# Two phases of four samples with both layers each, in a two-layer kernel on one core

## The reference

```
# layer 0 ("layer A")
h = einsum('bij,bkj->bik', x, weight0[adapter0])     # one 1024x1024 matrix per sample
h = layernorm(h) * gamma + beta
h = fake_quant(h) @ fake_quant(w1).T + b1            # int8 grid, scale per row
h = gelu(h)
x = x + fake_quant(h) @ fake_quant(w3).T + b3
# layer 1 ("layer B")
y = x @ base_w.T + bias + scale[a] * (x @ A[a].T) @ B[a].T      # rank 16
n = y * rsqrt(mean(y*y) + eps)
res, pre, post = heads(n)                            # 16 + 4 + 4 logits per token
H = (1 - g) * I + g * sinkhorn(res, 50 iterations, tau 0.1)     # 4x4 per token
branch = sum_s softmax(pre)[s] * y[s] @ W_branch     # y as 4 streams of 256
x = x + H mixed over the 4 streams of y + branch * softmax(post)
```

## Time and profile before

| | |
|---|---|
| median of three runs | 876.65 us (874.74 to 877.16) |
| the profiled execution's own time | 874.75 us |
| its span in the trace | 872.8 us |
| mean granted TensorE clock, share of full speed | 0.954 |
| TensorE busy | 761.2 us (87%) |
| VectorE busy | 578.2 us (66%) |
| ScalarE busy | 335.4 us (38%) |
| GpSimd busy | 64.7 us (7%) |

### The profile page before, as it was taken

One profiled execution on the slowest core, in us unless ns is written; L12 is line 12 of the kernel. 1 busy time (PEld: TensorE's weight loads), 2 busy tenths in 40 slices (PEclk: granted clock), 3 DMA queues, 4 the chain that ended last, 5 costly groups with the idle time before them and its releaser, 6 DMA issues.

```text
span 872.8 us, 11055 instructions
## 1 busy us (share of the span) xinstructions
PE 761.2 (87%) x3172; PEld 488.5 (56%) x3172; DVE 578.2 (66%) x2036; ACT 335.4 (38%) x577; POOL 64.7 (7%) x34
## 2 busy tenths in 40 slices
PE   4989899989899999998968899999898892699656
PEld 2544444344444444444645788887687771587445
DVE  6555282434675656483746524438999998899998
ACT  0333733304534252434324633444333421757152
POOL 0002000202621011022020000000000000000000
PEclk9999999989999999999999899999999996899969
DMA  8994654133448353512031345334333249653103
GB/s 340 374 334 163 240 179 171 60 111 140 159 149 355 108 189 139 193 56 89 24 121 50 129 161 182 115 114 159 122 128 108 102 155 411 272 193 121 48 35 158
DMA packets 40297, 140.94 MB, mean 161 GB/s; under 512 B 8511, under 2 KB 9663, under 8 KB 34626
## 3 DMA queue, kind: packets, MB, share of 16 engines
q1 hardware_dynamic: 38962, 137.72, 43.8%
q10 hardware_dynamic: 1296, 2.74, 0.8%
HBM read 106.86 MB, written 33.58 MB: 161 GB/s over the span
## 4 chain that ended last, share of the span: by engine, by line
PE 49%; DVE 34%; ACT 8%; issue 5%; DMA 2%; POOL 1%; DVEq 0%; SPq 0%; ACTq 0%
PE PS L779 21%; PE PS L837 12%; PE PS L947 8%; DVE ksum L1361 6%; DVE kprod L1356 6%; DVE ka L1365 4%; DVE nr L1438 4%; DVE kb L1365 3%; PE PS L826 2%; ACT qT L542 2%; DVE xr L1283 2%; PE PS L868 2%; DMA x_raw<-x_tr_dram 2%; PE PS L794 1%; DVE xp L1268 1%
## 5 line engine op out<-in xcount | busy, mean ns | idle before, releaser
L779 PE MATMUL PS<-w_raw,x_raw 128*128 128x512 f32 x512 | 230.4, 604 | 13.7 <-DMA x_raw<-x_tr_dram 11.0
L779 PEld LDWEIGHTS PS<-w_raw,x_raw 128*128 128x128 f32 x512 | 96.7, 194 | 124.9 <-issue 124.1
L947 PE MATMUL PS<-w_hi,xT_hi 128*128 128x512 f32 x256 | 105.0, 410 | 0.0
L947 PE MATMUL PS<-w_lo,xT_hi 128*128 128x512 f32 x256 | 102.0, 399 | 0.0
L947 PE MATMUL PS<-w_hi,xT_lo 128*128 128x512 f32 x256 | 101.7, 397 | 0.0
L1361 DVE TENSOR_REDUCE ksum<-kprod 128x16 f32<-128x64 f32 x392 | 75.2, 233 | 0.2 <-issue 0.2
L837 PE MATMUL PS<-w3q,qT 128*128 128x512 bf16 x256 | 61.3, 395 | 14.4 <-ACT qT L542 14.4
L1131 DVE SCALAR_TENSOR_TENSOR gbuf<-PS,lnst,vecs 128x512 f32<-128x512 f32 x32 | 23.7, 749 | 75.0 <-PE PS L837 75.0
L542 ACT ACTIVATE qT<-PS,round_c 128x512 bf16<-128x512 f32 x64 | 40.3, 679 | 84.4 <-PE PS L826 84.3
L837 PE MATMUL PS<-w1q,qT 128*128 128x512 bf16 x256 | 60.4, 391 | 8.4 <-DVE x1buf L1149 5.7
L470 POOL TENSOR_TENSOR xres<-xres,vecs 128x1024 f32<-128x1024 f32 x16 | 42.2, 2659 | 329.8 <-DMA xres<-x_tok_dram 329.8
(11 more groups left out here) (165 smaller groups left out, 1128.2 us busy)
## 6 DMA issues: line engine op xcount, KB each, us to landing
w_raw<-cond_w_dram SPq DMA_DIRECT2D x32, 1024.0 KB, 5.6
stage<-w_dram SPq DMA_DIRECT2D x16, 512.0 KB, 12.1
x_raw<-x_tr_dram SPq DMA_DIRECT2D x32, 256.0 KB, 6.4
xres<-x_tok_dram SPq DMA_DIRECT2D x8, 1024.0 KB, 9.3
x_scratch<-x1buf SPq DMA_DIRECT2D x16, 512.0 KB, 6.4
x1n<-x_scratch SPq DMA_DIRECT2D x16, 512.0 KB, 5.7
xr<-x_scratch SPq DMA_DIRECT2D x16, 512.0 KB, 3.6
y_scratch<-y SPq DMA_DIRECT2D x16, 512.0 KB, 3.6
```

What stands on the lines that cost most here:

```text
L779: mm = pe.matmul(PS[:, 2 * t + h, :], x_raw[pr][:, c, t * P:(t + 1) * P], w_raw[pr][:, c, h * H2:(h + 1) * H2], start=(pr == 0 and c == 0) ...
L947: pe.matmul(PS[:, 2 * t + h, :], xx[:, c, t * P:(t + 1) * P], ws[c // 2][:, c % 2, h * H2:(h + 1) * H2], start=(c == 0 and xx is xT_hi and ...
```

## The change

The eight samples are processed as two phases of four, each with layer A, an entry and layer B (`PHASES`). What follows from that:

- **Turn.** After layer B step 3 the kernel goes back to layer A with sample 4. Before the first entry the quantised matrices `w1q` and `w3q` are stored to DRAM (`store_quantised`), and loaded again at the turn. Blocks of samples 4 and 5 are loaded as buffers of layer B come free, in the order of pairs 2, 0, 1, 3 (`ORDER`).
- **Second entry.** Samples 6 and 7 drain as before; the first entry is a copy of it with samples 2 and 3.
- **Sinkhorn of group 0** starts at the turn: 11 iterations ahead of the first layer norm, three shares of four in layer A step 5, three of three in each of steps 6 and 7, two at a time in layer B step 4. Layer B steps 5 to 7 have none. The tiles that Sinkhorn uses move to memory that layer A doesn't use.
- **Two orientations.** `kmat_t` holds the transposed matrices, and the column half of an iteration reads them, so that it multiplies and reduces with the same access pattern as the row half.
- `base_w` is loaded and split one step earlier (`GUEST`), the products of the head weights with `base_w` and the LoRA matrices (`composites_1`, `composites_2`) come one step earlier, `av_hi` and `av_lo` have 56 columns and not 128, and all loops are written out straight.

```diff
+    PHASES = ((0, HALF), (HALF, NB))
+    GUEST = 3
...
+    ORDER = (2, 0, 1, 3)
...
+        kmat_t = [sb(f"kmat_t{i}", [P, HG, NS, NS], F32) for i in range(2)]
...
+            def store_quantised():
+                sp.wait_ge(st_ev, 2 * NW)
+                for i, wq in ((0, w1q), (1, w3q)):
+                    sp.dma_start(wq_dram[i], wq[:, :, :].rearrange("p c n -> p (c n)")).then_inc(wq_st, 16)
...
+            def enter_b(ph):
+                first, end = PHASES[ph]
+                sp.wait_ge(l0_pair, PAIRS * end - 1)
...
+                    load_x1n(first, t)
+                store_x1(end - 2, 0)
+                store_x1(end - 2, 1)
+                load_xres(end - 1)
...
+                    load_x1n(first + 1, t)
+                sp.wait_ge(b_set, ph + 1)
...
+            sp.wait_ge(xt_done, 4 * HALF)
+            load_blocks(HALF, 2)
+            step_b(HALF - 1, last=True)
+            sp.wait_ge(l1_done, 4 * HALF)
+            sp.wait_ge(lg_done, HALF)
+            load_x(HALF, 2)
+            load_blocks(HALF, 0)
+            load_x(HALF, 0)
+            load_blocks(HALF, 1)
+            load_x(HALF, 1)
+            load_x(HALF, 3)
+            store_y(HALF - 1)
+            for t in range(NTOK):
+                sp.wait_ge(y_st[t], 16 * HALF)
+            sp.wait_ge(ss_done, NTOK * HALF)
+            load_blocks(HALF, 3)
+            load_w(HALF + 1, 2)
+            sp.wait_ge(wq_st, 32)
+            sp.wait_ge(br_done, HALF)
+            sp.dma_start(w1q[:, :, :].rearrange("p c n -> p (c n)"), wq_dram[0]).then_inc(w1_back, 16)
+            load_w(HALF + 1, 0)
+            store_r(HALF - 1)
+            for t in range(NTOK):
+                sp.wait_ge(r_st[t], 16 * HALF)
+            sp.dma_start(w3q[:, :, :].rearrange("p c n -> p (c n)"), wq_dram[1]).then_inc(w3_back, 16)
+            load_w(HALF + 1, 1)
+            load_w(HALF + 1, 3)
...
-                if pr == 0:
+                order = ORDER if s == HALF else range(PAIRS)
+                pe.wait_ge(wld[pr], 32 * s + 32 + (16 if s >= GUEST else 0))
+                if s == HALF and pr == order[0]:
+                    pe.wait_ge(y_ev, 4 * HALF)
+                elif pr == order[0]:
                     wait(pe, l0_evac, NTOK * s)
...
+            l0(HALF, ORDER[0])
+            branch_transposes(HALF - 1)
+            l0(HALF, ORDER[1])
+            branch(HALF - 1)
+            l0(HALF, ORDER[2])
+            l0(HALF, ORDER[3])
+            step_a(HALF + 1, w3_=False)
+            for s in range(HALF + 2, NB):
+                step_a(s)
+            enter_b(1)
+            for b in range(HALF + 1, NB):
...
+                for i in range(2):
+                    nc.vector.tensor_tensor(kmat_t[i][:, :, :, :].rearrange("p t j i -> p t i j"), hr[:, chain[i], :, :],
+                                            cols(ska[:, 1, chain[i], :], HG), ALU.mult).then_inc(k_step[i], 1)
...
+            def half(k, row):
+                vec, new = (kb, ka) if row else (ka, kb)
+                for i in range(2):
+                    v = vec[i][:, :, :]
+                    dve.wait_ge(k_step[i], k)
+                    nc.vector.tensor_tensor(kprod[i][:, :, :, :], (kmat if row else kmat_t)[i][:, :, :, :], cols(v, HG),
+                                            ALU.mult).then_inc(k_step[i], 1)
+                for i in range(2):
+                    dve.wait_ge(k_step[i], k + 1)
+                    nc.vector.tensor_reduce(ksum[i][:, :, :], kprod[i][:, :, :, :], AX.X, ALU.add).then_inc(k_step[i], 1)
+                for i in range(2):
+                    dve.wait_ge(k_step[i], k + 2)
+                    nc.vector.reciprocal(new[i][:, :, :], ksum[i][:, :, :]).then_inc(k_step[i], 1)
...
-            def half(k, row):
...
-                    nc.vector.tensor_tensor(kprod[i][:, :, :, :], kmat[i][:, :, :, :], cols(v, HG) if row else rows(v, HG),
-                                            ALU.mult).then_inc(k_step[i], 1)
...
-                    pr = kprod[i][:, :, :, :]
...
-                    nc.vector.tensor_reduce(ksum[i][:, :, :], pr if row else pr.rearrange("p t i j -> p t j i"),
-                                            AX.X, ALU.add).then_inc(k_step[i], 1)
...
+            done = [0]
+            def share(n):
+                n = min(n, SINKHORN - 1 - done[0])
+                iterations(0, done[0], n)
+                done[0] += n
+            def step_a(s, w1_=True, w3_=True, n=0):
+                if w1_:
+                    layer_norm(s - 1, 0)
...
-            def step_b(b, first=False, last=False, sink=False):
-                def share(i):
-                    if sink:
-                        n = B_ITERS // 4
-                        iterations(0, (b - NB // 2) * B_ITERS + i * n, n)
...
+                share(n)
+                if w3_:
+                    finish_w3(s - 2, 0)
+                if w1_:
+                    layer_norm(s - 1, 1)
+                if w3_:
+                    finish_w3(s - 2, 1)
+                share(n)
+                if w1_:
+                    finish_w1(s - 1, 0)
+                for first, end in PHASES:
+                    if s == end - 1:
+                        lo_xT(first, 0)
+                        lo_xT(first, 1)
+                share(n)
+                if w1_:
+                    finish_w1(s - 1, 1)
...
+            for s in range(2, HALF):
+                step_a(s)
+            enter_b(0)
+            layer_b(0)
             sinkhorn_start(0)
-            with dve.Fori(NB // 2, NB - 1) as b:
-                step_b(b, sink=True)
-            step_b(NB - 1, last=True, sink=True)
-            iterations(0, NB // 2 * B_ITERS, SINKHORN - 1 - NB // 2 * B_ITERS)
+            share(11)
+            step_a(HALF + 1, w3_=False, n=4)
+            for s in range(HALF + 2, NB):
+                step_a(s, n=3)
+            enter_b(1)
+            step_b(HALF, first=True, n=2)
+            share(SINKHORN)
             sinkhorn_finish(0)
+            for b in range(HALF + 1, NB):
+                step_b(b, last=b == NB - 1)
             lo_xp(NB - 1)
             distribute(NB - 1)
             sinkhorn_start(1)
-            with dve.Fori(0, (SINKHORN - 1) // 7) as it:
-                iterations(1, it * 7, 7)
+            iterations(1, 0, SINKHORN - 1)
```

More of the change, by code:

```diff
@@ new lines, in _ @@
+            load_stage(KC + 5)
+            load_w(1, 2)
+            load_scales(0, V_SW1)
+            load_stage(KC + 6)
+            load_stage(KC + 7)
+            load_w(1, 3)
+            load_xres(0)
+            for c in range(4):
+                load_nat(c)
+            load_w(2, 0)
+            for c in range(4, KC):
+                load_nat(c)
+            load_w(2, 1)
+            store_scales(1)
+            load_w(2, 2)
+            load_scales(1, V_SW3)
+            load_w(2, 3)
@@ new lines, in drain_a @@
+            def drain_a(end):
+                evac_T(end - 2, 0, 3)
+                ln_root(end - 1, 0)
+                quant1(end - 1, 0)
+                evac_T(end - 2, 1, 3)
+                evac_T(end - 1, 0, 1)
+                ln_root(end - 1, 1)
+                quant1(end - 1, 1)
+                evac_T(end - 1, 1, 1)
+                for t in range(NTOK):
+                    gelu(end - 1, t)
+                    quant2(end - 1, t)
+                for t in range(NTOK):
+                    evac_T(end - 1, t, 3)
@@ L1059, in mix @@
                 mm.then_inc(pm_done, 1)
+            for pr in range(PAIRS):
+                l0(0, pr)
+                stage_T(2 * pr)
+                stage_T(2 * pr + 1)
+            l0(1, 0)
+            stage_T(KC)
+            stage_T(KC + 1)
+            l0(1, 1)
+            stage_T(KC + 2)
+            stage_T(KC + 3)
+            transposes(0, 0, 1)
+            product(0, 0, 1)
+            l0(1, 2)
+            stage_T(KC + 4)
+            stage_T(KC + 5)
+            transposes(0, 1, 1)
@@ new lines, in enter_b @@
+            def enter_b(ph):
+                first, end = PHASES[ph]
+                pe.wait_ge(wlo_done, PAIRS)
+                base(first, 0, 0)
+                transposes(end - 2, 0, 3)
+                product(end - 2, 0, 3)
+                base(first, 0, 1)
+                transposes(end - 2, 1, 3)
+                product(end - 2, 1, 3)
+                transposes(end - 1, 0, 1)
+                product(end - 1, 0, 1)
+                base(first, 1, 0)
+                transposes(end - 1, 1, 1)
+                product(end - 1, 1, 1)
+                base(first, 1, 1)
+                for t in range(NTOK):
+                    transposes(end - 1, t, 3)
+                    product(end - 1, t, 3)
+                low_and_heads(first)
+                for t in range(NTOK):
+                    for h in range(2):
+                        low_rank(first, t, h)
+                heads(first)
+                x_transposes(first + 1, 0)
+                x_transposes(first + 1, 1)
@@ L1397, in step_b @@
```

(1 more changed line is left out.)

742 lines of the change are left out of this document (347 added, 395 removed).

## The result

The changed kernel takes 912.77 us (median of four runs, 911.1 to 913.54) against 875.69 us for the kernel before in the same comparison (872.34 to 877.16). The ratio is 1.0426, 95% interval 1.0391 to 1.0462: slower, as forecast. The profiled execution has a span of 909.3 us, 36.5 more than before; the sum had 26.4.

What follows compares the result with a forecast made beforehand. TensorE bounds layer A, VectorE's chain the tail; gains must come from layer B's second half, tail or an entry. Terms summed to +26.4 on span 872.8, 899.2; with 1.95 outside and 1.9 to the median, 903 us, range 889 to 914.

Steps and rivals of the forecast that it cites:

- The entry and its last step: Added entry into layer B plus phase 0's own last A step, copies of those measured: 73.4 + 6.2 = 79.6 us.
- the likeliest case: Whole kernel: the forecast itself, 903 us, with range 895 to 908 and chance 0.63.
- the heavier case: Rival, 908 to 920, chance 0.16: GpSimd lock (908), or column half gains nothing and gaps remain 1.3 (910).
- VectorE's free 18 us are in the right gaps: Layer A steps 6 and 7: nine iterations fit, only the share after lo_xT in step 7 costs, 0.9 (0 to 4).
- The turn: Layer B step 3's end back to layer A: a chain of 87.0 us, replacing two A steps of 92.0.
- slow restarts of the forecast: Turn: matmuls run slower after TensorE idles, 8.8 instead of 7.0 for l0(4, 2) and 1.8 more for a product.
- Loads due later than they land: nothing: Turn: loads of w1q, w3q and sample 5 cost nothing, unless the queue is a few us slower than 406.
- Had the iterations been free, as in that rival: Rival: group 0's 49 iterations cost no time anywhere, turn 18.1 less, 879.0 us; chance 0.07 (872 to 885).
- The transfer ahead of x1: Layer A step 3: x1n queues behind stores including wq_scratch, so transposes wait 6.0 us (0 to 7.5).
- The shares in the second entry: Second entry with layer B step 4: Sinkhorn shares delay lo_xT, gather and lo_stacks, 5.0 us (3 to 8).
- The tail: After layer B: 7.9 ahead of the iterations, 4.3 from kmat_t and 1.3 from straight code saved, 0.4 for writes.
- The lock as a rival: Layer A step 7: GpSimd's second add holds share multiplies back 5.3 us, giving 908; within the heavier rival's 0.16.

Runs made afterwards that it cites:

- order experiment: Changed kernel with ScalarE's layer-norm square root placed behind the evacuation for the w3 product in layer A steps 5 to 7: 901.85 us, ratio 1.0324.
- load put forward: Changed kernel with 48 of group 0's 49 iterations left out and the load of sample 5's second pair issued earlier at the turn: 884.32 us, ratio 1.0106.
- early store: Changed kernel with the two wq_scratch stores issued a step and a half earlier, behind sample 2's last load: 904.89 us, ratio 1.0355.
- three small parts of it: Kernel before with transposed matrices, the tail's loop written out and lo_xp of sample 7 ahead of group 0's last iteration: 860.64 us, ratio 0.9829.

## Why the prediction was right, and where it was off

**The direction and its reason held.** The forecast was slower, for a second entry of 79.6 that buys back a layer B step, two layer A steps in part, and the Sinkhorn time. The entry and its last step measured 80.7, and with group 0's iterations nearly free the kernel still stood 1.7% above the one before. 912.77 lies in the range 889 to 914, but only 1.2 from its end and not in the likeliest case's own 895 to 908. It falls where I had the heavier case, 908 to 920, and for neither of the two mechanisms named there. That it is still inside the range is partly luck.

**The step that failed: "VectorE's free 18 us are in the right gaps".** The sum gave 0.9 for nine iterations in each of layer A steps 6 and 7; it was 10.4. I had checked that a share ends before TensorE wants its PSUM banks, which asks only about TensorE, the engine that VectorE serves directly. What I had not followed is the third engine: ScalarE's program puts the square root of a layer norm ahead of an evacuation for TensorE, so a share that delays the layer norm delays that too. At the turn I had named exactly this, and did not carry it on to the next steps. The order experiment takes 10.9 off these two steps and leaves VectorE's work alone, so this is shown.

**The turn**, 87.0 against 83.0: the chain was the right one. In the execution of the table, matmuls after the first wait ran at 7.1 for a pair and not 8.8, iterations at 1.62 and not 1.64, the product behind `qT` near full speed. Two other executions of the same turn had 9.9 for that pair, 5.0 for the product, and 86.8 and 87.1 in all, so the slow restarts of the forecast were neither right nor wrong: both happen. "Loads due later than they land: nothing" was wrong by its own reading: the load of sample 5's second pair came 4.3 late. It cost nothing only because VectorE's chain ended later still. Had the iterations been free, as in that rival, 879 would not have come out but 889.6. The load put forward takes 5.3 of these 10.6 (884.32); of the rest, 4.0 are in the turn (72.9 against the 68.9 of that rival) and 2.2 in the wait for `x1n`.

**The transfer ahead of x1**: mechanism right, size 8.2 for 6.0 (the bound of 7.5 was too low as well). The early store takes all of it. **The shares in the second entry**: 8.6 for 5.0 (range 3 to 8). One iteration instead of all brings the entry from 79.8 to 74.6. How the rest divides between its shares and those behind step 7's `lo_xT` was not tried.

**The tail**: 14.6 for 13.1. 7.6 of it lie ahead of the iterations (7.5 forecast) and 7.0 in them (5.6 forecast). Of the 2.8 of small gaps I took half and all went. The price of a column half was right: the reductions, as the trace groups them, before and after (min, median, max in ns):

```profile
L1361 DVE TENSOR_REDUCE ksum<-kprod x392: 206/234/272, 600.1 to 836.2; 128x16 f32<-128x64 f32 x196
```

```profile
L1396 DVE TENSOR_REDUCE ksum<-kprod x392: 203/211/218, 434.1 to 872.7; 128x16 f32<-128x64 f32 x196
```

The strided ones, up to 272, are gone; every one now is like the row half's.

**The lock as a rival** was there and small. That rival had the second add of step 7 meet a share. The adds of that step, from GpSimd's timeline after:

```profile
547.52 5.65 POOL L528 TENSOR_TENSOR xres<-xres,vecs 128x1024 f32<-128x1024 f32 x2 [46.87 <-DMA xres<-x_tok_dram]
576.89 4.66 POOL L528 TENSOR_TENSOR xres<-xres,vecs 128x1024 f32<-128x1024 f32 x2 [23.72 <-DMA xres<-x_tok_dram]
```

The second began after the share's last instruction (575.43) and met none of its multiplies. The first ran to 553.17 and met a layer norm and the start of a share; VectorE's timeline after:

```profile
552.51 0.88 DVE L1392 TENSOR_TENSOR kprod<-kmat,kb 128x64 f32<-128x64 f32 x2
...
553.85 0.35 DVE L1392 TENSOR_TENSOR kprod<-kmat_t,ka 128x64 f32<-128x64 f32 x2
```

One pair of multiplies took 0.88 for 0.35. That is 0.5 and not 5.3, since the add was nearly over. (The 2.66 that the rival gives for one instruction of an add is not what the rows show either: two take 5.65.) The Trainium skill (SBUF — State Buffer, section Who interferes with whom) has it that of two such instructions the one that starts later is blocked until the other has ended; the trace agrees in kind, and the price here was what was left of GpSimd's instruction. No run here removed the adds.

## What to carry to other kernels

Before giving an engine's idle time to other work, follow its outputs through every in-order engine behind it: work that fits between an engine's own deadlines can still hold a neighbour at an instruction, and with it what is queued behind that instruction. When a large change loses, take it apart: here three small parts of it, alone in the old kernel, gained 1.7%, and the large one was not brought even. A wait that is hidden by a longer one is still a wall; check how far below the first wall the next one stands before counting on the gain.

## What the runs showed of the hardware

A reduction over four values with a stride took up to 272 ns, one over neighbours 203 to 218, for the same shape (the iterations of the kernel before hold both kinds, those of the changed kernel only the second); the multiply took 0.35 us a pair either way. A loop on VectorE of seven rounds with seven iterations each cost 2.7 us more than the same code written out, 0.4 for a round, of which 0.3 shows in the trace as a longer gap at a round's end. Where TensorE waited less, its granted clock was higher: 0.99 instead of 0.96 in layer B steps 4 to 7 with the transposed matrices, and in layer A steps 6 and 7 the order experiment gave 10.9 us back for 8.3 of waits. The same matmuls behind the same wait of 3.2 to 3.5 ran at a granted clock of 1.00 in one execution (7.1 us for a pair) and of 0.74 in another (9.9 us).
